# Sixteen-head attention on one core: score products issued in front of the first product for maxima

## Chip, cores and metric

The kernel runs on one core of a Trainium2 chip. The metric is the device time of one execution in microseconds (us): the median of several runs.

## What is computed

Four layers, each an attention block and a feed-forward block with a gated residual, on 32 sequences of 100 positions with 128 channels; the attention reads a context of 1444 keys per sequence. Three of the four attentions have 16 heads of 8 channels. Cut to what matters:

```python
x = x + tanh(g_xattn[0]) * L0_xattn(layernorm(x), ctx)          # first stage, 16 heads
x = x + tanh(g_ffn[0])   * L0_ffn(layernorm(x))
x = x + tanh(g_xattn[1]) * L1_xattn(ctx, layernorm(x), mask)    # second stage, 16 heads, mask
x = x + tanh(g_ffn[1])   * L1_ffn(layernorm(x))
x = x + tanh(g_xattn[2]) * L2_xattn(layernorm(x), ctx, mask)    # one head, another function
x = x + tanh(g_ffn[2])   * L2_ffn(layernorm(x))
x = x + tanh(g_xattn[3]) * L3_xattn(layernorm(x), ctx, lengths) # last stage, 16 heads, lengths
x = x + tanh(g_ffn[3])   * L3_ffn(layernorm(x))

# a 16-head attention: q, k, v projected, split into heads
scores = einsum('bhqd,bhkd->bhqk', q, k) * scale      # masked where there is a mask
attn   = softmax(scores, axis=-1)
out    = einsum('bhqk,bhkd->bhqd', attn, v)           # heads joined, output projection
```

## The kernel before

Each layer is a phase of its own with one hand-written instruction stream per engine, tied by semaphores. Two functions hold the 16-head attention: `attention_phase` (the second stage, with a mask) and `packed_attention_phase` (the first stage and the last, the last with lengths). Both loop over the 32 sequences b, called batches here, and in a batch over 24 units u: two halves of eight heads, each times 12 tiles of 128 keys (the twelfth has 36).

The softmax needs the maximum of each query's scores ahead of the exponentials, and computes the scores twice. The first time (`max_mm`, weight loads and matmuls at L878 and L1635) queries lie on the partitions and up to 482 keys in the free dimension; VectorE reduces each product to a column of maxima (`reduce_max`, L696, L1482, L1475). This runs 16 units ahead of the rest (LEAD). When the maxima of a half are complete, `negate_max` turns them into negated maxima by a few small VectorE steps (L709 to L717, L1490 to L1494), `neg_turn` transposes them on TensorE (L863, L1621), VectorE copies them to SBUF (`neg_copy`, L728, L1511) and POOL spreads them into the rows 96 to 127 of `qblk` (L469, L1288, L1291). The second time (`score_mm`, L891 with the mask product L895, and L1662) keys lie on the partitions, and the product already has the maximum subtracted; ScalarE takes the exponential (L562, L1370, L1372), and in every even unit `pv_mm` (L907, L1674) adds the value products of the two units before. POOL also makes the low parts of the next keys and queries (L445, L450, L1257, L1262) and spreads the queries (L459, L1271); these follow ScalarE's `q_round` (L529, L1341), which stands ahead of the exponentials of unit 20.

Two rings in PSUM order TensorE. Scores and the projections of keys and values share two slots (`slot`): each waits until the second job before it has been read by ScalarE. Products for maxima share three buffers (`ring`) with the small jobs: `q` (query projection, unit 18), `neg` (units 9 and 21), `out` (transposes of the output, unit 2), `concat` (unit 5), `wo` (output projection, unit 8), in the masked stage `u` (unit 13), in the packed stages `left` (L1649; units 8, 12, 16, behind the value products). A job waits until VectorE has counted up `mx_free` for the third job before it. VectorE takes all of them in the order of the ring: `normalise` (L750 to L757, L1521 to L1525) reads `out`, `concat_copy` (L769, L1535, L1537) reads `concat`, `update_x` (L773, L1541) reads `wo`; at unit 3 it also makes the mask row of the next batch (`mask_rows`, L674, L1460).

In the masked stage every unit has two products for maxima, `max_mm(2 * g)` and `max_mm(2 * g + 1)`. In the packed stages 128 query columns go into each, so an even unit has two (`fulls[0]`, `fulls[1]`) and an odd unit one. TensorE's order in a unit before the change: first product for maxima, the two score products, the small job if the unit has one, second product for maxima, value products in even units, `left`, projections.

Of the kernel before, what the change touches and what calls it, by code (L numbers as in the profile page):

```python
# [33 lines left out]
def bc(ap, axis, n):  # L34

    ap = ap.unsqueeze(axis)
    shape = list(ap.shape)
    shape[axis] = n
    return ap.broadcast_to(shape)
# [155 lines left out]
def attention_phase(nc, name, x, xnT, ident, w, dram, scale, gate, mask=None, lens=None):  # L195

    with ExitStack() as ctx:
# [616 lines left out]
        def _(pe):  # L814
            def ring(*job):

                wait_some(pe, mx_free, mx_turn[job] - RING + 1)
                return p_ring(*job)

            def slot(*job):  # L820

                wait_some(pe, sc_free, sc_turn[job] - 1)
                return p_slot(*job)
# [42 lines left out]
            def max_mm(k):  # L866
                b, r = divmod(k, 2 * UNITS)
                if b >= B:
                    return
                h, r = divmod(r, 2 * KT)  # L870
                head, c = divmod(r, NCH)
                o, n = CHUNKS[c]
                if r == 0:
                    pe.wait_ge(stack_in[b % 2][h], (b // 2 + 1) * 96)
                    pe.wait_ge(qblk_ready, 2 * b + h + 1)
                to = ring("max", k)
                g = 2 * h + head // 4
                pe.matmul(to[0:S, 0:n], qblk[0:96, b % 2, HALF * h + head, :], stack[0:96, b % 2, g, o:o + n],  # L878
                          start=True, stop=True).then_inc(mx_full, 1)

            def score_mm(b, u):
                h, kt = divmod(u, KT)
                r = D if kt < KT - 1 else LAST
                if kt == 0:
                    pe.wait_ge(qneg_ready, 2 * b + h + 1)
                if u == 0 and mask is not None:
                    pe.wait_ge(pen_ready, b + 1)
                to = slot("exp", UNITS * b + u)
                for g in range(2):
                    out_ = to[0:r, g, 0:4 * S]  # L890
                    ins = pe.matmul(out_, stack[:, b % 2, 2 * h + g, kt * D:kt * D + r],  # L891
                                    qblk[:, b % 2, HALF * h + 4 * g:HALF * h + 4 * g + 4, :].rearrange("p h s -> p (h s)"),
                                    start=True, stop=mask is None)
                    if mask is not None:
                        ins = pe.matmul(out_.rearrange("p (h s) -> p h s", h=4), identb[0:r, 0:r],  # L895
                                        bc(pen[0:r, b % 2, kt, :], 1, 4), start=False, stop=True)
                ins.then_inc(sc_full, 1)
# [15 lines left out]
            def out_turn(b):  # L913
                to = ring("out", b)
                pe.wait_ge(pv_out, 2 * b + 2)
                for a in range(2):
                    for h in range(2):
                        ins = pe.transpose(to[0:S, a * 256 + h * D:a * 256 + (h + 1) * D],
                                           osb[:, h, a * S:(a + 1) * S], ident[:, :])
                ins.then_inc(mx_full, 1)  # L920
# [44 lines left out]
            for b in range(B):  # L965
                for u in range(UNITS):
                    g = UNITS * b + u + LEAD
                    max_mm(2 * g)
                    score_mm(b, u)
                    if b > 0:  # L970
                        if u == OUT_AT:
                            out_turn(b - 1)
                        if u == CONCAT_AT:
                            concat_turn(b - 1)
                        if u == WO_AT:
                            out_proj(b - 1)
                    if u == NEG1_AT:
                        neg_turn(b, 1)
                    if u == U_AT and mask is not None and b + 1 < B:
                        u_proj(b + 1)  # L980
                    if u == Q_AT and b + 2 < B:
                        q_proj(b + 2)
                    if u == NEG0_AT and b + 1 < B:
                        neg_turn(b + 1, 0)
                    max_mm(2 * g + 1)
                    if u % 2 == 0 and (b > 0 or u > 0):
                        for back in (2, 1):
                            at = UNITS * b + u - back
                            pv_mm(at // UNITS, at % UNITS)
                    if u == V01_AT and b + 1 < B:  # L990
                        v_proj("v01", b + 1)
                    if u == V2_AT and b + 1 < B:
                        v_proj("v2", b + 1)
                    if u == K0_AT and b + 2 < B:
                        k_proj("k0", b + 2)
                    if u == K12_AT and b + 2 < B:
                        k_proj("k12", b + 2)
# [24 lines left out]
def packed_attention_phase(nc, name, x, xnT, ident, w, dram, scale, gate, lens=None):  # L1022


    with ExitStack() as ctx:
# [101 lines left out]
        def fulls_at(b, u):  # L1127

            k = MAX_JOBS * 2 * b + PACKED_LEAD + u + (u + 1) // 2
            return (k, k + 1) if u % 2 == 0 else (k,)  # L1130

        def job_of(k):

            b, r = divmod(k, 2 * MAX_JOBS)
            return ("max", b) + (r // MAX_JOBS, r % MAX_JOBS // NCH, r % NCH) if b < B else None
# [447 lines left out]
        def _(pe):  # L1583
# [40 lines left out]
            def max_mm(job):  # L1624
                if job is None:
                    return
                _, b, h, block, c = job
                o, n = CHUNKS[c]
                if block == 0 and c == 0:
                    pe.wait_ge(stack_in[b % 2][h], (b // 2 + 1) * 96)  # L1630
                    pe.wait_ge(qblk_ready, 2 * b + h + 1)
                to = ring(*job)
                g, j = 2 * h + block // PACKED, block % PACKED
                at = 4 * S * g + D * j
                pe.matmul(to[:, 0:n], qblk[0:96, b % 2, at:at + D], stack[0:96, b % 2, g, o:o + n],  # L1635
                          start=True, stop=True).then_inc(mx_full, 1)
# [16 lines left out]
            def score_mm(b, u):  # L1653
                h, kt = divmod(u, KT)
                r = D if kt < KT - 1 else LAST
                if kt == 0:
                    pe.wait_ge(qneg_ready, 2 * b + h + 1)
                to = slot("exp", UNITS * b + u)
                for g in range(2):
                    out_ = to[0:r, g, 0:4 * S]  # L1660
                    at = 4 * S * (2 * h + g)
                    ins = pe.matmul(out_, stack[:, b % 2, 2 * h + g, kt * D:kt * D + r], qblk[:, b % 2, at:at + 4 * S],  # L1662
                                    start=True, stop=True)
                ins.then_inc(sc_full, 1)
# [68 lines left out]
            for b in range(B):  # L1733
                for u in range(UNITS):
                    fulls = fulls_at(b, u)
                    max_mm(job_of(fulls[0]))
                    score_mm(b, u)
                    if b > 0:
                        if u == OUT_AT:
                            out_turn(b - 1)  # L1740
                        if u == CONCAT_AT:
                            concat_turn(b - 1)
                        if u == WO_AT:
                            out_proj(b - 1)
                    if u == NEG1_AT:
                        neg_turn(b, 1)
                    if u == Q_AT and b + 2 < B:
                        q_proj(b + 2)
                    if u == NEG0_AT and b + 1 < B:
                        neg_turn(b + 1, 0)  # L1750
                    for k in fulls[1:]:
                        max_mm(job_of(k))
                    if u % TOGETHER == 0 and (b > 0 or u > 0):
                        for back in range(TOGETHER, 0, -1):
                            at = UNITS * b + u - back
                            pv_mm(at // UNITS, at % UNITS)
                    left_mm(left_of(b, u))
                    if u == V01_AT and b + 1 < B:
                        v_proj("v01", b + 1)
                    if u == V2_AT and b + 1 < B:  # L1760
                        v_proj("v2", b + 1)
                    if u == K0_AT and b + 2 < B:
                        k_proj("k0", b + 2)
                    if u == K12_AT and b + 2 < B:
                        k_proj("k12", b + 2)
# [2218 lines left out]
```

## Time and profile before

| | |
|---|---|
| median of 3 runs | 5812.44 us (5808.93 to 5820.26) |
| the profiled execution | 5809.02 us, span 5807.2 us |
| mean granted TensorE clock | 0.953 of full speed |
| busy: TensorE matmul, weight load | 5269.3 us (91%), 3460.8 us (60%) |
| busy: VectorE, ScalarE, POOL | 3857.1 us (66%), 3098.6 us (53%), 1590.2 us (27%) |
| first stage | about 47 to 1410 us |
| second stage | about 1706 to 3450 us |
| last stage | about 4394 to 5720 us |

The span runs from the first to the last instruction. A busy TensorE isn't TensorE at its peak, since matmuls are pipelined and their ends are modelled; the starts of weight loads (PEld) are the better clock of its progress. Idle time in front of an instruction, in brackets in the rows, matters only on the engine that is the bound of a stage. The usual gap in a load row after value products is about 0.3 us, whatever the row names as its cause.

### The profile page before, as it was taken

What the parts mean: (1) busy time and instruction counts of PE and PEld (TensorE: products, weight loads), DVE (VectorE), ACT (ScalarE), POOL (GpSimd) and SP (SyncE); (2) the same over time, 40 slices, a digit from 0 to 9 for tenths busy, and PEclk for the clock granted to TensorE, in tenths of its full rate; (3) what the DMA queues carried; (4) which work ended last, traced back from release to release, by engine and by line L of the source; (5) the groups of instructions that cost most, each with busy time, mean ns of one, the idle gap of its engine ahead of it and who ended that gap; (6) DMA issues with size and microseconds to landing.
All of it is one profiled execution on the core that took longest, in us unless ns stands there. A gap on an engine that the chain in (4) does not pass through costs nothing. (4 is left out here: it accounts for less than half of the span.)

```text
span 5807.2 us, 109944 instructions
## 1 busy us (share of the span) xinstructions
PE 5269.3 (91%) x39878; PEld 3460.8 (60%) x39878; DVE 3857.1 (66%) x10948; ACT 3098.6 (53%) x4492; POOL 1590.2 (27%) x1360
## 2 busy tenths in 40 slices
PE   7999999997959999999999988979458999999996
PEld 4666666665835555555555547857355666666663
DVE  6666666665766666666666667746466666667674
ACT  4666666665624444444444445634145666666664
POOL 3222222221442222222222214500352222222220
PEclk9999999998979999999999989989579999999998
DMA  3333323232233332332332315378333333323230
GB/s 88 77 75 72 79 70 78 68 73 61 62 101 74 81 79 73 81 79 74 83 79 73 77 40 112 74 200 254 84 95 70 75 70 72 74 69 77 68 73 13
DMA packets 160602, 475.40 MB, mean 82 GB/s; under 512 B 34720, under 2 KB 85723, under 8 KB 159866
## 3 DMA queue, kind: packets, MB, share of 16 engines
q1 hardware_dynamic: 148738, 449.69, 32.4%
q0 software_dynamic: 11328, 18.72, 1.1%
q8 instruction: 318, 5.21, 0.4%
q14 instruction: 218, 1.79, 0.1%
HBM read 237.66 MB, written 19.88 MB: 44 GB/s over the span
## 5 line engine op out<-in xcount | busy, mean ns | idle before, releaser
L696 DVE CUSTOM_DVE_ANT_0 a_dump<-a_max,a_mqf 100x482 f32<-100x482 f32 (+1 forms) x1536 | 978.8, 657 | 426.0 <-PE a_max L878 395.0
L1482 DVE CUSTOM_DVE_ANT_0 a_dump<-a_max,a_penq 128x482 f32<-128x482 f32 (+3 forms) x1248 | 783.1, 656 | 403.9 <-PE a_max L1635 382.9
L1475 DVE TENSOR_REDUCE a_mx<-a_max 128x1 f32<-128x482 f32 (+3 forms) x1248 | 779.8, 654 | 397.0 <-PE a_max L1635 273.7
L1635 PE MATMUL a_max<-a_stack,a_qblk 96*128 96x482 f32 (+1 forms) x2304 | 1027.7, 447 | 13.2 <-DVE a_mx L1482 8.5
L562 ACT ACTIVATE a_probs<-a_scores 128x800 f32<-128x800 f32 (+1 forms) x768 | 643.3, 838 | 657.1 <-PE a_scores L895 656.9
L1370 ACT ACTIVATE a_probs<-a_scores,a_kbias 128x800 f32<-128x800 f32 (+1 forms) x768 | 696.9, 926 | 404.2 <-PE a_scores L1662 404.2
L1662 PE MATMUL a_scores<-a_qblk,a_stack 128*128 128x400 f32 (+1 forms) x3072 | 832.2, 353 | 39.9 <-POOL a_qblk L1291 33.3
L1372 ACT ACTIVATE a_probs<-a_scores 128x800 f32<-128x800 f32 (+1 forms) x768 | 624.7, 836 | 410.2 <-PE a_scores L1662 406.1
L878 PE MATMUL a_max<-a_stack,a_qblk 96*100 96x482 f32 (+1 forms) x1536 | 711.1, 483 | 40.5 <-DVE a_mx L696 27.6
L1674 PE MATMUL a_pv<-a_probs,a_v_aug 128*32 128x200 f32 x12288 | 705.7, 341 | 3.0 <-ACT a_probs L1370 2.1
L1662 PEld LDWEIGHTS a_scores<-a_qblk,a_stack 128*128 128x128 f32 (+1 forms) x3072 | 548.1, 184 | 184.6 <-POOL a_qblk L1291 57.2
L1635 PEld LDWEIGHTS a_max<-a_stack,a_qblk 96*128 96x128 f32 x2304 | 434.8, 189 | 281.3 <-issue 104.7
L891 PE MATMUL a_scores<-a_qblk,a_stack 128*128 128x400 f32 (+1 forms) x1536 | 549.9, 413 | 0.9 <-POOL a_qblk L469 0.9
L895 PE MATMUL a_scores<-a_pen,a_identb 128*128 128x400 bf16 (+1 forms) x1536 | 528.1, 344 | 0.0
L1674 PEld LDWEIGHTS a_pv<-a_probs,a_v_aug 128*32 128x32 f32 x12288 | 298.6, 108 | 325.2 <-issue 216.6
L1288 POOL TENSOR_TENSOR a_qblk<-a_nsb,a_blk 32x768 fp32r<-32x768 f32 x128 | 187.9, 1468 | 934.7 <-DVE a_nsb L1511 930.0
L1257 POOL TENSOR_TENSOR a_klo<-a_kf,a_khi 128x1444 fp32r<-128x1444 f32 x64 | 211.0, 3296 | 831.5 <-ACT a_khi L1334 417.2
L878 PEld LDWEIGHTS a_max<-a_stack,a_qblk 96*100 96x100 f32 x1536 | 257.1, 169 | 251.0 <-DVE a_mx L696 148.9
L907 PE MATMUL a_pv<-a_probs,a_v_aug 128*32 128x200 f32 x6144 | 349.8, 340 | 0.4 <-ACT a_probs L562 0.4
L895 PEld LDWEIGHTS a_scores<-a_pen,a_identb 128*128 128x128 bf16 (+1 forms) x1536 | 147.0, 96 | 297.3 <-issue 296.5
L891 PEld LDWEIGHTS a_scores<-a_qblk,a_stack 128*128 128x128 f32 (+1 forms) x1536 | 290.4, 189 | 38.9 <-issue 28.1
L445 POOL TENSOR_TENSOR a_klo<-a_kf,a_khi 128x1444 fp32r<-128x1444 f32 x32 | 104.9, 3277 | 602.0 <-ACT a_khi L523 601.8
(554 smaller groups left out, 8471.2 us busy)
## 6 DMA issues: line engine op xcount, KB each, us to landing
a_stack<-a_khi SPq DMA_DIRECT2D x768, 180.5 KB, 3.4
a_ctxT<-in_ctxT_dram SPq DMA_DIRECT2D x128, 722.0 KB, 11.1
a_stack<-a_klo SPq DMA_DIRECT2D x384, 180.5 KB, 3.5
f_wb<-weights_by_token SPq DMA_DIRECT2D x16, 1600.0 KB
a_ctxn<-in_ctxn_dram SPq DMA_DIRECT2D x32, 704.0 KB
a_mt_i<-in_mask1T_dram SPq DMA_DIRECT2D x32, 600.0 KB, 7.0
a_mq_i<-in_mask_dram SPq DMA_DIRECT2D x32, 564.1 KB
a_mask_i<-in_mask_dram SPq DMA_DIRECT2D x32, 541.5 KB
```

The costliest lines, as they stand in the source:

```text
L562: act.activation(out_, in_, ACT.Exp, scale=scale).then_inc(sc_free, 1)
L696: nc.vector.tensor_tensor_reduce(dump[:, k % 2, 0:n], src, mqf[:, b % 2, o:o + n], 1.0, -3.0e38, ALU.mult, ALU.max, out_).then_inc(mx_free, 1)
L878: pe.matmul(to[0:S, 0:n], qblk[0:96, b % 2, HALF * h + head, :], stack[0:96, b % 2, g, o:o + n], start=True, stop=True).then_inc(mx_full, 1)
L891: ins = pe.matmul(out_, stack[:, b % 2, 2 * h + g, kt * D:kt * D + r], qblk[:, b % 2, HALF * h + 4 * g:HALF * h + 4 * g + 4, :].rearrange( ...
L895: ins = pe.matmul(out_.rearrange("p (h s) -> p h s", h=4), identb[0:r, 0:r], bc(pen[0:r, b % 2, kt, :], 1, 4), start=False, stop=True)
L1370: act.activation(out_, in_, ACT.Exp, bias=kbias[0:rows, b:b + 1, kt], scale=scale).then_inc(sc_free, 1)
L1372: act.activation(out_, in_, ACT.Exp, scale=scale).then_inc(sc_free, 1)
L1475: nc.vector.tensor_reduce(out_, src, AX.X, ALU.max).then_inc(mx_free, 1)
L1482: nc.vector.tensor_tensor_reduce(dump[0:rows, k % 2, 0:n], src, penq[0:rows, b % 2, o:o + n], 1.0, -3.0e38, ALU.add, ALU.max, out_).then_i ...
L1635: pe.matmul(to[:, 0:n], qblk[0:96, b % 2, at:at + D], stack[0:96, b % 2, g, o:o + n], start=True, stop=True).then_inc(mx_full, 1)
L1662: ins = pe.matmul(out_, stack[:, b % 2, 2 * h + g, kt * D:kt * D + r], qblk[:, b % 2, at:at + 4 * S], start=True, stop=True)
L1674: ins = pe.matmul(p_pv[32 * t:32 * t + 32, 0:2 * S], v_aug[0:r, b % 2, kt, head:head + 2, :].rearrange("p h d -> p (h d)"), probs[0:r, u % ...
```

## The change

In both functions the TensorE stream of a unit issues the two score products ahead of the first product for maxima instead of behind it. The orders of VectorE, ScalarE, POOL and the DMA queue are as before, and so are the orders in which ring buffers and slots are given out, since scores and maxima come from different rings.

```diff
@@ attention_phase, block.tensor
             for b in range(B):
                 for u in range(UNITS):
                     g = UNITS * b + u + LEAD
+                    score_mm(b, u)
                     max_mm(2 * g)
-                    score_mm(b, u)
                     if b > 0:
                         if u == OUT_AT:
                             out_turn(b - 1)
@@ packed_attention_phase, block.tensor
             for b in range(B):
                 for u in range(UNITS):
                     fulls = fulls_at(b, u)
+                    score_mm(b, u)
                     max_mm(job_of(fulls[0]))
-                    score_mm(b, u)
                     if b > 0:
                         if u == OUT_AT:
                             out_turn(b - 1)
```

## Rows read from the trace of the kernel before

**Rows 1.** Page, costliest groups: line, engine, operation, shapes, count, busy, mean, idle before.
```profile
L696 DVE CUSTOM_DVE_ANT_0 a_dump<-a_max,a_mqf 100x482 f32<-100x482 f32 (+1 forms) x1536 | 978.8, 657 | 426.0 <-PE a_max L878 395.0
L562 ACT ACTIVATE a_probs<-a_scores 128x800 f32<-128x800 f32 (+1 forms) x768 | 643.3, 838 | 657.1 <-PE a_scores L895 656.9
```
**Rows 2.** Busy time in two stretches: a batch of the second stage, one of the first.
```profile
core 0: us, PE busy (x) PEld busy (x) DVE busy (x) ACT busy (x) POOL busy (x), PEclk, DMA share, GB/s
2380.11:2434.37 54.26, 53.16 (x410) 30.32 (x409) 36.87 (x120) 26.65 (x37) 13.89 (x10) 1.00 0.32 78
386.27:427.07 40.80, 40.38 (x341) 26.49 (x340) 27.62 (x56) 25.10 (x35) 11.22 (x12) 1.00 0.32 74
```
**Rows 3.** Timeline (start, us, engine, instruction, idle before), first stage, unit 0.
```profile
395.10 0.30 PEld L1662 LDWEIGHTS a_scores<-a_qblk,a_stack 128*128 128x128 f32 x2 [0.79 <-POOL a_qblk L1291]
395.39 0.19 PEld L1635 LDWEIGHTS a_max<-a_stack,a_qblk 96*128 96x128 f32 x1
396.00 0.66 DVE L1475 TENSOR_REDUCE a_mx<-a_max 128x1 f32<-128x482 f32 x1 [0.62 <-PE a_max L1635]
```
**Rows 4.** Timeline, first stage, units 5 and 6.
```profile
402.08 0.19 PEld L1635 LDWEIGHTS a_max<-a_stack,a_qblk 96*128 96x128 f32 x1 [0.32 <-issue]
402.61 0.66 DVE L1475 TENSOR_REDUCE a_mx<-a_max 128x1 f32<-128x482 f32 x1 [0.38 <-PE a_max L1635]
403.32 0.19 PEld L1635 LDWEIGHTS a_max<-a_stack,a_qblk 96*128 96x128 f32 x1
```
**Rows 5.** Timeline of weight loads, second stage, unit 4, and its last units without maxima.
```profile
2393.16 0.16 PEld L878 LDWEIGHTS a_max<-a_stack,a_qblk 96*100 96x100 f32 x1 [0.87 <-DVE a_mx L696]
2394.56 0.16 PEld L878 LDWEIGHTS a_max<-a_stack,a_qblk 96*100 96x100 f32 x1 [0.45 <-DVE a_mx L696]
...
3448.35 0.11 PEld L891 LDWEIGHTS a_scores<-a_qblk,a_stack 128*36 128x36 f32 x1 [0.32 <-issue]
3448.65 0.09 PEld L895 LDWEIGHTS a_scores<-a_pen,a_identb 36*36 36x36 bf16 x1 [0.19 <-issue]
```
**Rows 6.** Timeline, last stage, units 2 to 8.
```profile
4691.07 0.65 DVE L1482 CUSTOM_DVE_ANT_0 a_dump<-a_max,a_penq 128x480 f32<-128x480 f32 x1
...
4696.30 0.19 PEld L1635 LDWEIGHTS a_max<-a_stack,a_qblk 96*128 96x128 f32 x1 [0.44 <-DVE a_mx L1482]
4696.88 0.19 PEld L1635 LDWEIGHTS a_max<-a_stack,a_qblk 96*128 96x128 f32 x1
...
4701.20 0.63 PEld L1649 LDWEIGHTS a_max<-a_stack,a_qleft 96*64 96x64 f32 x4 [0.74 <-issue]
```
**Rows 7.** Timeline, second stage, units 7 to 9.
```profile
2399.81 0.20 PEld L891 LDWEIGHTS a_scores<-a_qblk,a_stack 128*128 128x128 f32 x1
2400.18 0.35 PEld L878 LDWEIGHTS a_max<-a_stack,a_qblk 96*100 96x100 f32 x2
2400.96 0.66 DVE L696 CUSTOM_DVE_ANT_0 a_dump<-a_max,a_mqf 100x482 f32<-100x482 f32 x1 [0.29 <-PE a_max L878]
2401.68 0.16 PEld L878 LDWEIGHTS a_max<-a_stack,a_qblk 96*100 96x100 f32 x1
...
2403.06 0.16 PEld L878 LDWEIGHTS a_max<-a_stack,a_qblk 96*100 96x100 f32 x1 [0.50 <-DVE a_mx L696]
```
**Rows 8.** Timeline, second stage, the negated maxima at unit 19, unit 22, and the first batch.
```profile
1723.50 0.98 DVE L711 CAST a_nmsp<-a_nm 100x8 fp32r<-100x8 f32 x1
...
2432.67 0.88 DVE L712 TENSOR_TENSOR a_nmsp<-a_nm,a_nmsp 100x8 fp32r<-100x8 f32 x1
2432.48 1.05 POOL L450 TENSOR_TENSOR a_qs<-a_qf,a_qs 32x400 fp32r<-32x400 f32 x1 [3.21 <-ACT a_qs L529]
2433.61 1.66 POOL L459 TENSOR_TENSOR a_qblk<-a_qs,a_blk 96x400 fp32r<-96x400 f32 x2
2435.42 0.16 PEld L878 LDWEIGHTS a_max<-a_stack,a_qblk 96*100 96x100 f32 x1 [0.42 <-DVE a_mx L696]
```
**Rows 9.** Timeline, first stage, VectorE and POOL at unit 19.
```profile
389.92 0.17 DVE L1494 TENSOR_TENSOR a_nmsp<-a_nm,a_nmsp 128x7 fp32r<-128x7 f32 x1
390.52 1.04 POOL L1262 TENSOR_TENSOR a_qs<-a_qf,a_qs 32x400 fp32r<-32x400 f32 x1 [2.24 <-ACT a_qs L1341]
```

## Prediction

> **What bounds the kernel now.** I read the page's table of groups first, then busy time by stage, then the timelines of weight loads, VectorE and POOL through one batch of each stage the diff touches. The whole batches of a stage repeat to a few hundredths of a us, so a loss per batch times their number is the loss of the stage. Three stages run a changed loop: the first (packed, 47 to 1410 us), the second (masked, 1706 to 3450) and the last (packed, with lengths, 4394 to 5720); the rest of the span is untouched. In them TensorE is the bound: in one batch of the first stage it is busy 40.38 of 40.80 us, in one of the second 53.16 of 54.26, against 27.62 and 36.87 for VectorE [rows 2]. The large idle times of the page are VectorE waiting for maxima (395.0 us in the second stage) and ScalarE waiting for scores (656.9) [rows 1]; neither engine is the bound, so they cost nothing by themselves.
>
> Short names: f0 is a unit's first product for maxima, S its two score products, f1 its second (in packed stages only even units have one), P the value products, which end every even unit. Before: f0 S f1 P, then f0 S (f1). After: S f0 f1 P, then S f0 (f1). Products for maxima share a ring of three PSUM buffers with the small jobs (out, concat, wo, neg, q, left): each waits until the third job before it has been reduced by VectorE.
>
> **What costs nothing.** Nothing is added, and no DMA or other queue is passed. The loop is a cycle: from one S to the next the same products stand between, only f0 now lies behind the first S instead of in front of the second. So every wait that runs from scores to scores keeps its length. That holds for the longest one in the packed stages: S of unit 0 waits for POOL (0.79 us idle) [rows 3], whose chain begins with the exponentials of unit 19, five S earlier. Its f0 is no longer hidden in that wait, but unit 19's f0 has left the way to the chain's start, the same 0.2 us. After P the exposed weight load is that of scores instead of maxima; the count of exposed loads is the same.
>
> **What costs something** is the place of f0 against VectorE. After P, f0 was first and VectorE started 0.53 us after its load (402.08 to 402.61) [rows 4]. Now it stands behind S. In a packed stage that is 0.29 us for S (395.10 to 395.39) and 0.61 from the load behind S to VectorE (395.39 to 396.00) [rows 3]: 0.90 instead of 0.53, 0.37 later. In the masked stage S with its mask products takes 0.30 (3448.35 to 3448.65) [rows 5] and 0.37 (2399.81 to 2400.18), and VectorE starts 0.78 after the load (2400.18 to 2400.96) [rows 7]; the second reduction, 0.58 behind the first, starts 2.03 us after P's end where it started at 1.64: 0.39 later. In even units f0 was glued to the unit before; now VectorE gets it 0.38 to 0.40 later. In most units VectorE's idle time takes that up. It is lost where VectorE is the late one. Place by place, per batch:
>
> 1. *First stage, units 5 and 6.* Concat takes a ring slot in unit 5, so f1 of unit 6 needs f0 of unit 5. From a reduction's start to the load that waits for it is 0.71 us (402.61 to 403.32): that wait just closes today, 1.24 us behind P [rows 4]. After: 0.90 + 0.71 = 1.61, 0.36 later. 31 x 0.36 = 11.2 us.
>
> 2. *Last stage, units 2 to 6.* VectorE runs a closed chain here: f0 of unit 2 (4691.07), normalise, f1, a mask row, then the next reductions; f1 of unit 6 (4696.88) waits for it [rows 6]. The chain starts 0.38 later. S in front of f0 fills waits inside it, but the last product still waits for VectorE; an exposed load gives back 0.03. 31 x 0.35 = 10.9 us.
>
> 3. *Last stage, units 7 and 8.* After the next P, VectorE gets f0 of unit 7 another 0.37 later; behind it come the four small steps of the negated maxima, f0 of unit 8, and the left job that waits for that (4701.20, 0.74 us idle, of which 0.32 is the usual gap after P) [rows 6]. It has no slack. 30 x 0.37 = 11.1 us.
>
> 4. *Second stage, units 2 to 6.* The same chain with a longer normalise; f1 of unit 4 (2394.56, 0.45 us idle) [rows 5] waits for its end. Loss 0.40, and 0.05 for the products behind concat: 31 x 0.45 = 14.0 us.
>
> 5. *Second stage, units 7 to 9.* f1 of unit 8 needs f1 of unit 7. A load to VectorE takes 0.78, and VectorE's start to the waiting load 0.72: 1.50 together, exactly the 1.50 between those two loads (2400.18 to 2401.68) [rows 7], closed today without a wait. After, the reduction starts 0.39 later, and so does f1 of unit 8. Against it, f0 of unit 9 waits 0.18 beyond the usual gap (0.50 less 0.32) [rows 7] and will have S in front. Net 0.21, 30 x 0.21 = 6.3 us.
>
> 6. *Second stage, units 19 to 22.* Today VectorE's two-input step of the negated maxima takes 0.88 us (0.17 in the packed stages [rows 9]) and ends with POOL's operation: 2432.67 + 0.88 = 2433.55, POOL 2432.48 + 1.05 = 2433.53 [rows 8]. Afterwards VectorE is 0.38 later there and POOL, which follows the exponentials of unit 19, 0.20 earlier. Then the cast in front of it runs into POOL's operation (a row has such a cast held, 0.98 us) and the last small step into POOL's next pair (1.66 us for two) [rows 8]. The next reduction starts near 2434.27 instead of 2433.55, 0.72 later; S fills the wait of f0 in unit 22 (0.42 idle) [rows 8], and 0.35 remains: 31 x 0.35 = 10.9 us. Bounds: a gain of 0.33 if the last step isn't held, a loss of 1.2 if it and the two-input step are. I take the middle, since the kinds before the last are seen held.
>
> The Trainium skill (SBUF — State Buffer, section "Who interferes with whom") says that a VectorE instruction with two SBUF inputs, or a copy, cast or tensor_scalar in a two-port mode, is blocked for its whole length by a GpSimd operation that started first. The trace agrees for the first two kinds (0.88 and 0.98 us); no row shows a tensor_scalar held. By this rule the last step is held, as taken; if the rule failed for it, step 6 would be the gain of 0.33 and the sum 21 us less.
>
> 7. *Small terms* (exposed loads that give back 0.05, f1 of plain even units 0.03 late, scores of 36 columns): both signs, taken as 0, bounds 5 either way.
>
> **Sum:** 11.2 + 10.9 + 11.1 + 14.0 + 6.3 + 10.9 = 64.4 us. The profiled execution took 5809.0 us (span 5807.2 and 1.8 around it): 5873.4. It lay 3.4 below the median of 5812.4, inside the runs' spread. I predict 5873.
>
> **Rivals.**
> *A, the ring's waits are filled.* S runs while f0 waits for its buffer. Rows: idle before f0 of 0.87, 0.18 (beyond the gap) and 0.42 us per batch in the second stage, 0.44 in the last [rows 5 to 8]. Won in full: 31 x 1.91 = 59 us, 5750. Against: behind each stands an f1 or left job that waits for the same VectorE chain. It decides from the point where VectorE's chain ends before f1 is due, that is if normalise didn't start on f0's reduction. Chance 0.07. The Trainium skill (Perfetto Trace Analysis, "Optimization Strategy") speaks for this: make the dependencies of the busiest engine start sooner. Here sooner scores mean later maxima, and the rows show closed waits at the maxima alone.
> *B, no change.* VectorE's idle time, a third of a batch [rows 2], takes the later starts up everywhere: 5809 to 5812. Against: the two waits of steps 1 and 5, which close today with no slack. Chance 0.07.
> *C, more collisions with POOL.* In the packed stages the two-input step of unit 19 starts 0.60 us before POOL's operation (389.92, 390.52) [rows 9]. It moves 0.38 later, POOL 0.21 earlier: a tie within 0.02. If POOL is first, VectorE stands 1.04 us and the small job neg behind it; S of unit 0 comes 0.25 to 0.3 later: 62 x 0.28 = 17 us, 5890. With two steps held in the second stage (26 us more) 5916. Chance 0.26.
> *D, the wait of unit 0 exposes f0*, if its chain begins at neg and not at unit 19: 64 x 0.2 = 13 us, 5886. Against: POOL goes from one operation of the chain to the next without idling for neg. Chance 0.05.
> The forecast itself has 0.55. That the reorder isn't carried out can't be: products go out in program order.
>
> **How the numbers follow.** Low end: step 6 at its gain (-21), step 4 absent (-14): 5838. High end: C's first form and some of its second: 5905. That leaves out A, B and C's far end, 0.18. A measurement of this kernel tells about 0.2%, 12 us, from no change. Faster 0.07, same 0.08, slower 0.85.
>
> **What would show it.** Right: a batch of the first stage 0.3 to 0.4 us longer, of the second 1.0, of the last 0.7; a new wait for VectorE at f1 of unit 6 in the first stage; the left job's 0.74 grown to some 1.1; the two-input step of the second stage no longer at 0.88. Wrong: TensorE's waits for VectorE fall in total (A), or batches of equal length (B).

## The result

| kernel | time, us (median, range, runs) |
|---|---|
| before | 5814.4 (5808.9 to 5820.3, 4) |
| after | 5867.1 (5860.6 to 5871.2, 4) |

The ratio is 1.0093, with a 95% interval of 1.0081 to 1.0104: the change costs 0.9%, some 53 us. The profiled execution of the changed kernel took 5860.6 us (span 5858.8), 51.6 more than that of before.

The table of groups of the page after, in the columns of [rows 1]:

```profile
L696 DVE CUSTOM_DVE_ANT_0 a_dump<-a_max,a_mqf 100x482 f32<-100x482 f32 (+1 forms) x1536 | 954.3, 656 | 512.2 <-PE a_max L878 474.8
L562 ACT ACTIVATE a_probs<-a_scores 128x800 f32<-128x800 f32 (+1 forms) x768 | 643.3, 838 | 641.5 <-PE a_scores L895 637.1
L891 PEld LDWEIGHTS a_scores<-a_qblk,a_stack 128*128 128x128 f32 (+1 forms) x1536 | 288.5, 188 | 158.1 <-issue 96.1
L878 PEld LDWEIGHTS a_max<-a_stack,a_qblk 96*100 96x100 f32 x1536 | 257.9, 171 | 136.7 <-DVE a_mx L696 81.5
```

ScalarE waits less for scores (641.5 us against 657.1) and VectorE more for maxima (512.2 against 426.0), as the swap of S and f0 implies. Neither says that the kernel is slower. The busy time of one batch of each changed stage does (second, first, last; columns of [rows 2]):

```profile
2346.00:2401.16 55.16, 53.43 (x416) 31.02 (x409) 36.04 (x120) 26.64 (x37) 13.95 (x10) 1.00 0.32 77
390.90:431.96 41.06, 40.52 (x340) 26.48 (x340) 27.41 (x55) 25.02 (x34) 11.28 (x11) 1.00 0.32 73
4724.60:4767.06 42.46, 41.13 (x339) 26.12 (x339) 28.54 (x95) 26.97 (x35) 11.29 (x11) 1.00 0.31 71
```

The granted clock is 1.00 in both kernels, so TensorE itself isn't slower. A batch of the second stage grew from 54.30 to 55.16 us, of the first from 40.80 to 41.06, of the last from 41.83 to 42.46 (medians of the 31 distances from one out job to the next in the timeline of weight loads). From the first out job of a stage to its last, that is 25.3 + 8.3 + 19.5 = 53.1 us, all of the difference.

Where in a batch it arises is read from the same timeline. Each even unit ends with P. I took the start of every P against that of unit 0's P, as a median over the batches, in both kernels, and subtracted. What each place adds to the batch, us:

| P of unit | 2 | 4 | 6 | 8 | 10 | 12 | 14 to 20 | 22 | next 0 | sum |
|---|---|---|---|---|---|---|---|---|---|---|
| first stage | 0 | 0 | +0.31 | 0 | 0 | -0.08 | 0 | 0 | +0.03 | +0.26 |
| second | +0.18 | +0.15 | +0.02 | +0.39 | -0.16 | -0.06 | +0.12 | +0.26 | -0.05 | +0.85 |
| last | +0.18 | +0.02 | +0.11 | +0.37 | 0 | -0.07 | +0.01 | +0.11 | -0.08 | +0.64 |

The loss sits in a few places. Most of the others keep step with before, units 10 and 12 gain a little, and from unit 14 to 20 of the second stage +0.12 gathers in steps of 0.02 to 0.04. Two of the places, first in the first stage, units 5 and 6 (timeline of weight loads, then VectorE; f0 of unit 5 and its reduction, f1 of unit 6, P):

```profile
404.34 0.19 PEld L1635 LDWEIGHTS a_max<-a_stack,a_qblk 96*128 96x128 f32 x1
405.65 0.19 PEld L1635 LDWEIGHTS a_max<-a_stack,a_qblk 96*128 96x128 f32 x1 [0.42 <-DVE a_mx L1475]
406.07 0.16 PEld L1674 LDWEIGHTS a_pv<-a_probs,a_v_aug 128*32 128x32 f32 x8 [0.23 <-issue]
...
404.94 0.66 DVE L1475 TENSOR_REDUCE a_mx<-a_max 128x1 f32<-128x482 f32 x1 [0.60 <-PE a_max L1635]
```

VectorE starts on f0 0.60 us after its load, and f1 of unit 6 is loaded 0.71 after that start (404.94 to 405.65), as before [rows 4]. The load followed its predecessor at once in the kernel before; now it waits 0.42 us for VectorE. In the last stage the wait stands at f1 of unit 8, one job ahead of where I had put it:

```profile
4775.72 0.66 DVE L1482 CUSTOM_DVE_ANT_0 a_dump<-a_max,a_penq 128x482 f32<-128x482 f32 x1 [0.94 <-PE a_max L1635]
...
4776.44 0.19 PEld L1635 LDWEIGHTS a_max<-a_stack,a_qblk 96*128 96x128 f32 x1 [0.34 <-DVE a_mx L1482]
4778.09 0.62 PEld L1649 LDWEIGHTS a_max<-a_stack,a_qleft 96*64 96x64 f32 x4 [0.73 <-issue]
```

Then the second stage at unit 19, VectorE and POOL, against [rows 8]:

```profile
2396.37 0.51 DVE L711 CAST a_nmsp<-a_nm 100x8 fp32r<-100x8 f32 x1
2396.91 0.17 DVE L712 TENSOR_TENSOR a_nmsp<-a_nm,a_nmsp 100x8 fp32r<-100x8 f32 x1
2397.00 0.83 DVE L717 TENSOR_SCALAR a_nneg<-a_nm 100x8 f32<-100x8 f32 x1
...
2395.80 1.04 POOL L450 TENSOR_TENSOR a_qs<-a_qf,a_qs 32x400 fp32r<-32x400 f32 x1 [3.06 <-ACT a_qs L529]
2396.93 1.68 POOL L459 TENSOR_TENSOR a_qblk<-a_qs,a_blk 96x400 fp32r<-96x400 f32 x2
```

The cast starts 0.57 us after POOL's first operation and ends with it (2396.88 against 2396.84). The two-input step starts in POOL's pause of 0.09 us, 0.02 ahead of POOL's next operation, and takes 0.17. The tensor_scalar starts 0.07 after POOL's next operation and takes 0.83. In the kernel before the two-input step alone was held. This is so in nearly every batch. Each step runs 64 times in the stage, some 30 of them at unit 19, beside POOL's work on the next queries: the cast takes 0.50 to 0.53 in 29 of the 64, the tensor_scalar 0.83 in 29, the two-input step 0.17 in 63 (before: 0.88 to 0.90 in 30).

### The profile page after: what moved, and what is told of

It is laid out like the page before. It is cut to its first block and busy times, and to the rows that moved or that the text cites. A ratio compares the mean times of both kernels' runs of the same rounds, so it can differ in the third digit from the quotient of the medians.

```text
span 5858.8 us, 109944 instructions
## 1 busy us (share of the span) xinstructions
PE 5302.3 (91%) x39878; PEld 3491.7 (60%) x39878; DVE 3815.3 (65%) x10948; ACT 3102.4 (53%) x4492; POOL 1591.8 (27%) x1360
## 5 line engine op out<-in xcount | busy, mean ns | idle before, releaser
L696 DVE CUSTOM_DVE_ANT_0 a_dump<-a_max,a_mqf 100x482 f32<-100x482 f32 (+1 forms) x1536 | 954.3, 656 | 512.2 <-PE a_max L878 474.8
L562 ACT ACTIVATE a_probs<-a_scores 128x800 f32<-128x800 f32 (+1 forms) x768 | 643.3, 838 | 641.5 <-PE a_scores L895 637.1
L1662 PE MATMUL a_scores<-a_qblk,a_stack 128*128 128x400 f32 (+1 forms) x3072 | 920.3, 381 | 44.6 <-POOL a_qblk L1291 38.0
L1635 PE MATMUL a_max<-a_stack,a_qblk 96*128 96x482 f32 (+1 forms) x2304 | 834.4, 398 | 15.8 <-DVE a_mx L1482 2.6
L1662 PEld LDWEIGHTS a_scores<-a_qblk,a_stack 128*128 128x128 f32 (+1 forms) x3072 | 488.6, 184 | 378.3 <-issue 174.1
L878 PE MATMUL a_max<-a_stack,a_qblk 96*100 96x482 f32 (+1 forms) x1536 | 629.1, 463 | 45.7 <-DVE a_mx L696 38.0
L891 PE MATMUL a_scores<-a_qblk,a_stack 128*128 128x400 f32 (+1 forms) x1536 | 611.0, 453 | 1.3 <-POOL a_qblk L469 1.3
L891 PEld LDWEIGHTS a_scores<-a_qblk,a_stack 128*128 128x128 f32 (+1 forms) x1536 | 288.5, 188 | 158.1 <-issue 96.1
L878 PEld LDWEIGHTS a_max<-a_stack,a_qblk 96*100 96x100 f32 x1536 | 257.9, 171 | 136.7 <-DVE a_mx L696 81.5
```

The source lines that it names most:

```text
L562: act.activation(out_, in_, ACT.Exp, scale=scale).then_inc(sc_free, 1)
L696: nc.vector.tensor_tensor_reduce(dump[:, k % 2, 0:n], src, mqf[:, b % 2, o:o + n], 1.0, -3.0e38, ALU.mult, ALU.max, out_).then_inc(mx_free, 1)
```

## The experiments

In the tables "batch" is the median length in the first, second and last stage, from the profiled execution. The kernel before was timed again next to each group of experiments and had medians of 5812.0 us (the first two headings below), 5842.4 (the packed unit 0 and the later round) and 5838.1 (the chain's start and the picked units). So times of different groups are compared by their ratio to before alone. The order is changed unit by unit with this edit, in both loops; the experiments name the set:

```
+                    if u in SET:
+                        score_mm(b, u)
                     max_mm(2 * g)
-                    score_mm(b, u)
+                    if u not in SET:
+                        score_mm(b, u)
```

### A few places, or a cost in every unit

```
quiet_units: masked SET = all but (1, 2, 7, 19), packed SET = all but (1, 2, 5, 7)
late_units:  masked SET = (1, 2, 7, 19),         packed SET = (1, 2, 5, 7)
```

> Scores first in all units except four of each stage: masked stage 1, 2, 7, 19; packed stages 1, 2, 5, 7, which keep the old order. Theory (the loss sits in a few places where VectorE's chain is closed against the product that waits for it): all of the batch's lengthening goes; a batch of the first stage 40.75 us (before 40.80, after 41.06), of the second 53.8 to 54.3 (before 54.30, after 55.16), of the last 41.75 to 41.83 (before 41.83, after 42.46); the median some 20 us below before, 5775 to 5815. Rival (the new order costs something on TensorE in every unit, an exposed load or a gap): 20 of 24 units keep it, so about 43 of the 52 us between before and after stay, near 5855.

> The complement: scores first only in units 1, 2, 7, 19 of the masked stage and 1, 2, 5, 7 of the packed stages. Theory (a few places): the whole loss and more, as the small gains of the other units are missing: batches 41.1, 55.2 to 55.8, and 42.5, and a time of 5865 to 5895. Rival (a cost in every unit): 4 of 24 units, 8 to 9 us over before, near 5822, batches 40.84, 54.44 and 41.93.

| kernel | batch, us | time | ratio to before (95%) |
|---|---|---|---|
| before | 40.80, 54.30, 41.83 | 5812.0 | 1 |
| quiet_units | 40.76, 53.76, 41.77 | 5793.1 | 0.9972 (0.9963 to 0.9982) |
| late_units | 41.09, 55.68, 42.50 | 5890.7 | 1.0137 (1.0117 to 1.0158) |

The two are complements, and the signs are opposite: scores first in twenty units of each stage gains 16 us, in the other four it loses some 80. The rival (a cost of the order in every unit, +43 and +8) is out. By place, late_units shows the losses of the table above to a hundredth or two (+0.31 at unit 6 in the first stage; +0.18, +0.15, +0.38 and, at unit 22, +0.62 in the second; +0.18, +0.02, +0.11, +0.36 in the last), and quiet_units shows the gains: -0.08 and -0.07 at unit 12 of the packed stages, and -0.15, -0.05, -0.37 and -0.05 at units 10, 12, 22 and the next 0 of the second. The loss of 0.26 at unit 22 in the changed kernel is thus two effects, +0.62 from unit 19 and -0.37 from S in unit 22 (picked_units, below, has the -0.37 with none of units 19 to 21 changed).

### Is it VectorE that is late

```
                 src, out_ = p_ring("max", k)[0:S, 0:n], ...
+                n = 64      (masked; the same in front of reduce_max's src in the packed stages)
```

> Old order, but VectorE reads only the first 64 columns of each product for maxima; the maxima of the other columns are left out, so softmax is shifted by another number. VectorE then has a large reserve everywhere. It is the partner of the next run; alone: the waits of TensorE for maxima go, 5700 to 5790.

> The same 64-column reductions (the maxima of the other columns are left out here too) with scores first in all units. Theory (only a late VectorE makes the new order cost): the difference to the old order with short reductions is between -10 and +5 us. Rival (the order costs on TensorE itself): +40 to +55 us, as with full reductions.

| kernel | batch, us | time |
|---|---|---|
| short_reduce_old | 40.79, 52.56, 40.87 | 5714.7 (5712.0 to 5719.6) |
| short_reduce_new | 40.71, 52.64, 40.81 | 5706.5 (5704.5 to 5708.9) |

With a quick VectorE the new order is 8 us faster instead of 53 slower. What the order costs, it costs through a VectorE that is late with the reductions. POOL's hold alone isn't enough: in short_reduce_new the two-input step of the second stage still takes 1.04 to 1.07 us in 28 of 64, and no step of that stage grows by more than 0.03. The masked batch keeps +0.09 us, in steps of 0.02 to 0.03 behind nearly every P: the small terms of step 7. Their counterpart are the units with 36-column scores, -0.05 to -0.09 each. The page of the first shows a group of L697 (L696 moved by a line) with a mean of 224 ns instead of 657:

```profile
L697 DVE CUSTOM_DVE_ANT_0 a_dump<-a_max,a_mqf 100x64 f32<-100x64 f32 x1536 | 341.9, 224 | 910.2 <-PE a_max L879 880.6
```

### Where VectorE's chain begins

```
units_1_7:    SET = (1, 7) in all stages
units_2_5_19: masked SET = (2, 19), packed SET = (2, 5)
```

> Scores first only in units 1 and 7 of every changed stage. The prediction put the start of the early loss at f0 of unit 2 (steps 2 and 4) and the later one at f0 of unit 7 (steps 3 and 5). By it: nothing at units 2 to 6 in any stage, +0.37 us behind unit 7 in the last stage, +0.39 in the masked one, 0 in the first: batches 40.80, 54.69, 42.20. Rival: VectorE's chain starts a unit earlier, at f0 of unit 1; then the 0.31 to 0.33 of units 2 to 6 are here: 55.0 and 42.5.

> Scores first only in units 2 and 19 of the masked stage and 2 and 5 of the packed ones. By the prediction: first stage +0.31 us at unit 6 (step 1), last stage +0.31 by unit 6 (step 2), masked stage +0.33 by unit 4 (step 4) and +0.62 at unit 22, where S of unit 22 doesn't fill the wait (step 6): batches 41.11, 55.25, 42.14. Rival (the early loss belongs to unit 1): 41.11, 54.92, 41.83.

| kernel | batch, us | second stage by unit 2, 4 | last stage by unit 2, 4, 6 |
|---|---|---|---|
| late_units | 41.09, 55.68, 42.50 | +0.18, +0.15 | +0.18, +0.02, +0.11 |
| units_1_7 | 40.80, 55.00, 42.51 | +0.18, +0.15 | +0.18, +0.02, +0.12 |
| units_2_5_19 | 41.11, 55.28, 42.15 | 0, +0.31 | 0, +0.20, +0.12 |

Each of the two was executed once (5878.6 and 5890.8 us), so the reading rests on the batches, whose lengths and steps agree with late_units to a few hundredths. The first came out by the rival, the second by the prediction: unit 1 alone brings the whole early loss (+0.33 and +0.31), unit 2 alone brings it too (+0.31 and +0.32), and both together no more than either. The timeline of VectorE in the last stage shows why. Each fence begins with P of unit 0, then f0 of unit 1, f0 of unit 2, and the first step of normalise. The kernel before:

```profile
4772.47 0.16 PEld L1674 LDWEIGHTS a_pv<-a_probs,a_v_aug 128*32 128x32 f32 x8 [0.30 <-issue]
...
4774.12 0.66 DVE L1482 CUSTOM_DVE_ANT_0 a_dump<-a_max,a_penq 128x482 f32<-128x482 f32 x1 [0.69 <-PE a_max L1635]
...
4774.71 0.65 DVE L1482 CUSTOM_DVE_ANT_0 a_dump<-a_max,a_penq 128x480 f32<-128x480 f32 x1
...
4775.33 0.21 DVE L1521 RECIPROCAL a_rs<-a_max 100x8 f32<-100x8 f32 x1
```

units_1_7:

```profile
4827.05 0.16 PEld L1677 LDWEIGHTS a_pv<-a_probs,a_v_aug 128*32 128x32 f32 x8 [0.30 <-issue]
...
4829.07 0.66 DVE L1485 CUSTOM_DVE_ANT_0 a_dump<-a_max,a_penq 128x482 f32<-128x482 f32 x1 [1.07 <-PE a_max L1638]
...
4829.66 0.65 DVE L1485 CUSTOM_DVE_ANT_0 a_dump<-a_max,a_penq 128x480 f32<-128x480 f32 x1
...
4830.24 0.20 DVE L1524 RECIPROCAL a_rs<-a_max 100x8 f32<-100x8 f32 x1
```

units_2_5_19:

```profile
4845.86 0.15 PEld L1677 LDWEIGHTS a_pv<-a_probs,a_v_aug 128*32 128x32 f32 x7 [0.31 <-issue]
...
4847.52 0.66 DVE L1485 CUSTOM_DVE_ANT_0 a_dump<-a_max,a_penq 128x482 f32<-128x482 f32 x1 [0.71 <-PE a_max L1638]
...
4848.46 0.66 DVE L1485 CUSTOM_DVE_ANT_0 a_dump<-a_max,a_penq 128x480 f32<-128x480 f32 x1 [0.28 <-PE a_max L1638]
4849.05 0.20 DVE L1524 RECIPROCAL a_rs<-a_max 100x8 f32<-100x8 f32 x1
```

Normalise starts 2.86 us behind P before, 3.19 in either experiment. In the kernel before f0 of unit 1, f0 of unit 2 and normalise follow each other without idle time. A late product anywhere in that run moves its end by the same 0.33: in the first experiment the run starts late, in the second there is a hole of 0.28 in its middle. Delays on two links of one gapless run count once: no more shows with both than with one. For units 7 and 19, which lie apart, they add: units_1_7 with units_2_5_19 less the early loss once is 0.70 + 0.98 - 0.31 = 1.37, and late_units shows 1.38.

### The wait of unit 0 in the packed stages

```
packed_unit0:  packed SET = (0,)
packed_unit19: packed SET = (19,)
```

> Scores first only in unit 0 of the packed stages; that S is the one that waits for POOL (0.79 us in the kernel before). f0 was hidden in front of that wait and now stands behind it. Theory (the wait is a closed chain that begins at the exponentials of unit 19 and is not moved): both packed batches grow by about 0.2 us, 41.0 and 42.0, some 12 us in all, near 5824. Rival (nothing is exposed): 40.80 and 41.83 stay, 5812.

> Scores first only in unit 19 of the packed stages, so that the exponentials there, and POOL's operations behind them, come one product (0.2 us) earlier. Theory of the prediction (the chain to unit 0's wait begins here): the packed batches shrink by about 0.2 us, 40.6 and 41.6, some 12 us in all, near 5800. Rival D (the chain begins later, at the negated maxima): they stay at 40.80 and 41.83, 5812; together with the 12 us of unit 0 the full reorder would then cost 12 us that the prediction counted at nothing. A third outcome, +0.3 us and more, if VectorE's two-input step now starts behind POOL's operation.

| kernel | batch, us | ratio to before (95%) |
|---|---|---|
| packed_unit0 | 41.02, 54.30, 42.06 | 1.0023 (1.0011 to 1.0034) |
| packed_unit19 | 40.60, 54.29, 41.63 | 0.9978 (0.9968 to 0.9988) |

S of unit 0 in the two kernels, the same batch of the first stage:

```profile
439.75 0.30 PEld L1662 LDWEIGHTS a_scores<-a_qblk,a_stack 128*128 128x128 f32 x2 [1.06 <-POOL a_qblk L1291]
```
```profile
434.92 0.19 PEld L1662 LDWEIGHTS a_scores<-a_qblk,a_stack 128*128 128x128 f32 x1 [0.59 <-POOL a_qblk L1291]
```

The wait was 0.79 us before [rows 3], and 0.77 in this batch. Taking f0 from in front of it exposes 0.21 us, starting its chain one product sooner takes 0.19 out of it, and the full change does both. The price of zero was right as a sum of two parts of 12 to 13 us each; rival D, which has the first part alone, is out.

packed_unit19 also explains two small entries of the last stage in the table of places, +0.11 at unit 22 and -0.08 at the next 0. With unit 19 alone changed, P of unit 22 is 0.12 us late and the next P of unit 0 gets 0.32 back: in unit 22 f0 now waits for VectorE, 0.36 us instead of a gap of 0.20 before, and the wait for POOL takes the delay in.

```profile
4871.69 0.19 PEld L1635 LDWEIGHTS a_max<-a_stack,a_qblk 96*128 96x128 f32 x1 [0.36 <-DVE a_mx L1482]
```

### The collision with POOL

```
 (ScalarE's loop of the masked stage, L608)
-                    if u == Q_AT + 2 and b + 2 < B:
+                    if u == Q_AT + 3 and b + 2 < B:
                         q_round(b + 2)
```

after_late_round has this in the changed kernel, before_late_round in the kernel before.

> The changed kernel, with ScalarE's q round of the masked stage one unit later (in front of the exponentials of unit 21 instead of 20), which moves POOL's later pair away from VectorE's four small steps. Theory (step 6: VectorE's small steps lose 0.34 and 0.66 us in that stage to POOL's operations): the cast takes 0.17 and the tensor_scalar 0.17 again, the masked batch falls from 55.16 to 54.4 to 54.6 us, 17 to 24 us less, 5843 to 5850. Rival (those steps are hidden, the loss at unit 22 is f0's place alone): 55.16 stays, 5867.

> The kernel before with the same later q round in the masked stage. Theory (its 0.88 us two-input step is POOL's doing and reaches f0 of unit 22, which waits 0.42 us): that step 0.17 us, the masked batch 53.9 to 54.1 instead of 54.30, 6 to 13 us less, near 5802. Rival (hidden): 54.30, 5812.

| kernel | batch, us | ratio to before (95%) |
|---|---|---|
| after | 41.06, 55.16, 42.46 | 1.0093 (1.0081 to 1.0104) |
| after_late_round | 41.09, 54.38, 42.46 | 1.0060 (1.0042 to 1.0078) |
| before_late_round | 40.80, 53.76, 41.84 | 0.9967 (0.9958 to 0.9977) |

The second stage of after_late_round, VectorE's three steps and POOL's first operation:

```profile
2253.91 0.17 DVE L711 CAST a_nmsp<-a_nm 100x8 fp32r<-100x8 f32 x1
2254.11 0.17 DVE L712 TENSOR_TENSOR a_nmsp<-a_nm,a_nmsp 100x8 fp32r<-100x8 f32 x1
2254.20 0.17 DVE L717 TENSOR_SCALAR a_nneg<-a_nm 100x8 f32<-100x8 f32 x1
...
2254.52 1.03 POOL L450 TENSOR_TENSOR a_qs<-a_qf,a_qs 32x400 fp32r<-32x400 f32 x1 [4.23 <-ACT a_qs L529]
```

POOL now comes 0.32 us behind the last of them, and each takes 0.17. The masked batch is 0.78 us shorter than after's, all of it at unit 22; on the old order it is 0.54 shorter. The collision was on the path in both kernels. For the old order I had expected 0.2 to 0.4, from f0's wait of 0.42 in unit 22 alone. But f1 of unit 21 waited for the same run of reductions. The kernel before shows its load with a wait of its own, 0.58 us ahead of the load of f0 in unit 22 [rows 8]:

```profile
2434.84 0.16 PEld L878 LDWEIGHTS a_max<-a_stack,a_qblk 96*100 96x100 f32 x1 [0.33 <-DVE a_mx L696]
```

### A version that beats both

```
picked_units:      masked SET = (9, 11, 22, 23), packed SET = (11, 19)
picked_late_round: the same, and the later q round
```

> Scores first only where the runs so far show a gain: masked stage units 9, 11, 22, 23; packed stages units 11 and 19. Sum of the steps seen one by one: masked -0.15 (unit 9), -0.05 (11), -0.37 (22), -0.05 (23), packed -0.08 (11) and -0.20 (19): batches 40.5, 53.7 and 41.55; 31 x (0.62 + 0.28 + 0.27) = 36 us less than before, a ratio of 0.994. Rival (the gains are taken back when the losing units aren't changed, since they fill the same waits): less than half of it, over 0.997.

> The same with the later q round of the masked stage. That round alone gave 0.54 us per masked batch, unit 22's order 0.37; both work on f0's wait in unit 22, so they don't add. Theory: masked batch 53.5, 40 us less than before in all, 0.993. If they did add: 53.2, 0.9915.

| kernel | batch, us | time | ratio to before (95%) |
|---|---|---|---|
| before | 40.80, 54.30, 41.83 | 5838.1 | 1 |
| picked_units | 40.40, 53.66, 41.35 | 5791.9 | 0.9916 (0.9902 to 0.9931) |
| picked_late_round | 40.40, 53.46, 41.34 | 5782.6 | 0.9901 (0.9886 to 0.9916) |

Both beat both kernels, the second by 1.0%. The gains of the second stage came as summed (-0.16, -0.06, -0.37, -0.05), and with the later round 0.55 at unit 22, the value that the round has alone: the two cures are for one wait and don't add. In the packed stages unit 11 gave more than expected, -0.21 and -0.29 instead of -0.08. With unit 12 left in the old order S of unit 12 follows f0 without the gap of 0.17 us ("issue") that it has in the kernel before; why it has the gap there isn't settled. In the full reorder and in quiet_units, where unit 12 has the new order too, only 0.07 to 0.08 of this gain is left.

## Why the prediction held

The forecast of 5873 us lies 6 above the median of 5867.1, the sum of 64.4 us 11 above the 53.1 that the three stages show. That the time came out nearer than the sum is luck: I had added it to the profiled execution of before, 5809.0, which lies 5.4 below the median of 5814.4. The terms, in us:

| step | predicted per batch, sum | measured per batch, sum |
|---|---|---|
| 1 first stage, units 5 and 6 | 0.36, 11.2 | 0.31, 9.6 |
| 2 last stage, units 2 to 6 | 0.35, 10.9 | 0.31, 9.6 |
| 3 last stage, units 7 and 8 | 0.37, 11.1 | 0.37, 11.1 |
| 4 second stage, units 2 to 6 | 0.45, 14.0 | 0.35, 10.9 |
| 5 second stage, units 7 to 9 | 0.21, 6.3 | 0.39 - 0.16, 6.9 |
| 6 second stage, units 19 to 22 | 0.35, 10.9 | 0.62 - 0.37, 8.1 |
| 7 small terms | 0 | -0.05 + 0.01 - 0.03, -2.2 |

The measured column adds up to 54.0, since a median times 30 or 31 isn't exactly the sum over the batches.

The places came as forecast, most of the sizes a little smaller. Of the signs named beforehand, the batches grew by 0.26, 0.86 and 0.63 us (0.3 to 0.4, 1.0 and 0.7), the wait at f1 of unit 6 appeared and the two-input step left its 0.88; the left job's idle time didn't grow.

**Steps 1 and 2** had mechanism, place and, nearly, size. In units_1_7 the first reduction starts 0.37 us later against P (2.02 for 1.65), but the end of the run came only 0.31 to 0.33 later at the next P. In step 2 I put the start of the run at f0 of unit 2. It begins at f0 of unit 1, in front of which VectorE is still idle for 0.69 us: unit 1 alone gave the whole loss. The sum didn't suffer, since links of one run count once. Had I added a term for each unit that is late, I would have been 20 us too high.

**Step 3** had its size to the hundredth, but the sign that I had named for it didn't come: the left job's idle time stayed (0.73 us against 0.74). The job before it, f1 of unit 8, waits 0.34 us for VectorE, and that makes P, and all behind it, late. The step should have followed the ring back one job.

**Step 4** was mis-sized by 0.10. The 0.40 for the start of the chain became 0.33, as in step 2, and the 0.05 for the products behind concat is only 0.02 in the changed kernel and 0 in late_units.

**Step 5** was right: 0.39 late at unit 8, and S in front of f0 of unit 9 gives 0.16 back where I had taken 0.18.

**Step 6** held in all its parts: the two-input step back at 0.17, the cast and the tensor_scalar held instead. VectorE came 0.62 late at unit 22 where I had 0.72, and S gave back 0.37. My 0.35 is 0.72 less that 0.37, the time of S in [rows 7]; less the wait of 0.42, as the step reads, it would be 0.30. Before the prediction no row showed a tensor_scalar held; now it takes 0.83 us in 29 batches. The Trainium skill (SBUF — State Buffer, section "Who interferes with whom") counts it among the instructions that a GpSimd operation blocks if it started first. By this rule it is held; the trace agrees. Also by this rule an operation that starts ahead of GpSimd's isn't held: in the packed stages the two-input step now starts 0 to 0.03 us before POOL's operation in some 60 batches, and takes 0.17 in all of them; for VectorE the trace agrees here too. POOL's operation, which by the same rule would be blocked while VectorE's 0.17 us lasts, is only 0.01 to 0.04 longer, and no run here tells why.

**Rivals.** B (no change) is out by the times. C's first form, the tie in the packed stages, fell the other way:

```profile
392.25 0.17 DVE L1494 TENSOR_TENSOR a_nmsp<-a_nm,a_nmsp 128x7 fp32r<-128x7 f32 x1
...
392.25 1.06 POOL L1262 TENSOR_TENSOR a_qs<-a_qf,a_qs 32x400 fp32r<-32x400 f32 x1 [2.04 <-ACT a_qs L1341]
```

VectorE was first and nothing was lost. The 17 us that it would have cost weren't tried. Its second form didn't come either, with the two-input step at 0.17. A as a whole is out, but it is true in places: S in front of f0 wins 0.37 us in unit 22 and 0.16 in unit 9 of the second stage. That is what the picked kernels collect. D is out by the two experiments on it.

**A sign that misled.** I had written that a fall of TensorE's waits for VectorE would show the forecast wrong. They did fall, summed over all weight loads from 570.6 to 478.2 us, and it was right. The view of waits, before and then after (total, times, longest):

```profile
PEld a_max L878 <- DVE a_mx L696: 148.9, 419, 2.2
PEld a_max L863 <- DVE a_mx L696: 6.0, 32, 0.4
```
```profile
PEld a_max L878 <- DVE a_mx L696: 81.5, 162, 1.9
PEld a_max L863 <- DVE a_mx L696: 33.5, 61, 0.8
```

Behind each P the first load has the usual gap of 0.32 us, whatever it is. With f0 there, the gap was put down to VectorE in many units, as in this load of the kernel before; with S there it goes to "issue" or to ScalarE: the idle time before L891 is 158.1 us in the page after. So of the 257 waits that left the row of L878 many are that gap under another name, and the new waits at f1 are lost in its fall; at neg (L863) they show.

```profile
2395.76 0.16 PEld L878 LDWEIGHTS a_max<-a_stack,a_qblk 96*100 96x100 f32 x1 [0.32 <-DVE a_mx L696]
```
The length of a batch, and the starts of P in it, can't be relabelled in this way.

## What to carry to other kernels

When an order is changed on the busiest engine, follow what is now late to the engine that answers it and back to the instruction that waits for the answer: where that loop is closed today without idle time, any delay shows in full, and links of one gapless run count once. Then try the order place by place: the same swap was worth -0.37 us in one unit and +0.62 in another, and a reorder of all units sums gains and losses that can be had apart. Judge by the length of a repeated batch, not by totals of waits, which take a new name when another instruction stands at the gap.

## What the runs showed of the hardware

I hadn't expected how finely the hold by POOL depends on who starts first. In the packed stages a start of VectorE's two-input step 0 to 0.03 us ahead of POOL's operation cost VectorE nothing in any of the 60 batches, and POOL's operation then took 1.05 to 1.08 us instead of 1.03 to 1.05; in the second stage a start of the tensor_scalar 0.07 behind it cost 0.66 (0.83 instead of 0.17). That 60 batches of the changed kernel fall within 0.03 us of each other, and those of packed_unit19 and picked_units too, with VectorE behind by no more than 0.001 us in any, may be more than chance; no run here tells.
